# Local attention: the clip of the row sums becomes a maximum over pairs, and the token shift moves from VectorE to ScalarE and GpSimd

## The reference, cut to what matters

```python
def shift_token(t):                       # the upper 64 features come from the token before
    t1, t2 = jnp.split(t, 2, axis=-1)
    t2 = jnp.pad(t2, ((0, 0), (1, 0), (0, 0)))[:, :-1]
    return jnp.concatenate([t1, t2], axis=-1)

def l2norm(t):
    return t / jnp.clip(jnp.linalg.norm(t, axis=-1, keepdims=True), 1e-12)
...
h = shift_token(x)
qkv = h @ wqkv                            # 128 -> 3 x 512, 8 heads of 64
q = l2norm(q) * qs
k = l2norm(k) * ksc
q, k = rotary_xpos(q, k)
o = local_attention(q, k, v)              # windows of 64, each sees itself and the one before
x = x + o @ wo
```

## Time and profile before

| | |
|---|---|
| time of three runs, median (lowest to highest) | 1549.52 us (1544.6 to 1549.98) |
| the profiled execution | 1545.77 us, its span 1544.0 us |
| busy in the span | PE 1237.7 us (80%), DVE 1138.3 us (74%), ACT 865.4 us (56%), POOL 829.3 us (54%) |
| mean granted PE clock | 0.914 |

### The profile page before, as it was taken

How to read it: one execution, slowest core, us unless ns; L and a number is a source line. 1 busy time by engine, 2 the same in 40 slices (tenths; PEclk the granted TensorE clock), 3 DMA queues, 4 the chain that set the end, 5 groups by cost and what they waited for, 6 DMA issues and landing times. The chain is left out here.

```text
span 1544.0 us, 26296 instructions
## 1 busy us (share of the span) xinstructions
PE 1237.7 (80%) x7828; PEld 800.8 (52%) x7828; DVE 1138.3 (74%) x2560; ACT 865.4 (56%) x2259; POOL 829.3 (54%) x760
## 2 busy tenths in 40 slices
PE   6889999854228988479689988885877998898797
PEld 3333333353116877334257666663555766666465
DVE  1299999847118877356589999982658999999464
ACT  5623333243114544237578878783746887888664
POOL 0064344245750555541177767676746776777663
PEclk9999999967559999869889999997998999999999
DMA  3700000031120122130100000000000000000001
GB/s 113 251 1 0 1 0 1 0 104 44 49 90 1 42 63 65 47 120 1 50 1 3 2 1 1 0 1 1 1 22 1 2 2 2 1 1 1 1 1 55
DMA packets 35031, 44.06 MB, mean 29 GB/s; under 512 B 5621, under 2 KB 24978, under 8 KB 34913
## 3 DMA queue, kind: packets, MB, share of 16 engines
q1 hardware_dynamic: 30304, 34.27, 7.0%
q0 software_dynamic: 4608, 8.47, 1.7%
HBM read 22.65 MB, written 21.12 MB: 28 GB/s over the span
## 5 line engine op out<-in xcount | busy, mean ns | idle before, releaser
L1865 ACT ACTIVATE W<-W,nm 128x128 f32<-128x128 f32 x512 | 197.9, 393 | 0.0
L1648 POOL TENSOR_TENSOR W<-W,rden 128x512 f32<-128x512 f32 x128 | 133.0, 1040 | 117.7 <-DVE rden L1966 111.5
L1633 POOL TENSOR_TENSOR R<-R 128x512 f32<-128x512 f32 x128 | 162.6, 1292 | 34.8 <-DVE R L1936 34.8
L1936 DVE TENSOR_TENSOR R<-bank,tab 128x1024 f32<-128x1024 f32 x128 | 151.0, 1214 | 17.0 <-ACT sq L1831 13.1
L1959 DVE CUSTOM_DVE_ANT_0 W<-bank,mask_q,rn 128x128 f32<-128x128 f32 x512 | 146.3, 338 | 7.7 <-issue 4.2
L1194 POOL DMA_INDIRECT expert_rows<-Yt,xin x80 | 83.2, 1040 | 115.4 <-DVE Yt L1167 89.1
L1849 ACT ACTIVATE QK<-bank 128x512 f32<-128x512 f32 x128 | 75.5, 590 | 68.0 <-PE bank L1720 61.1
L616 DVE TENSOR_TENSOR_SCAN S<-beta,U 128x512 f32<-128x512 f32 x64 | 100.0, 1583 | 0.0
L1865 ACT ACTIVATION_READ_ACCUMULATOR W<-W,nm 128x1 f32 x512 | 98.5, 192 | 0.0
L1770 PE MATMUL bank<-PT,VA 128*64 128x128 f32 (+1 forms) x1024 | 86.3, 262 | 13.9 <-issue 10.9
L1745 PE MATMUL bank<-QK 64*64 64x128 f32 x2048 | 85.8, 282 | 11.6 <-DVE nm L1959 11.3
(11 more groups left out here) (310 smaller groups left out, 3583.3 us busy)
## 6 DMA issues: line engine op xcount, KB each, us to landing
expert_slots<-empty SPq DMA_DIRECT2D x8, 650.0 KB, 6.4
xin<-expert_slots SPq DMA_DIRECT2D x8, 650.0 KB
expert_rows<-empty SPq DMA_DIRECT2D x8, 512.0 KB, 6.7
pair_rows<-expert_rows SPq DMA_DIRECT2D x16, 256.0 KB, 4.2
expert_raw<-w1e_dram SPq DMA_DIRECT2D x9, 256.0 KB, 2.8
expert_raw<-w2e_dram SPq DMA_DIRECT2D x9, 256.0 KB, 3.0
tok<-x_dram SPq DMA_DIRECT2D x8, 256.0 KB, 4.5
out_dram<-tok_out SPq DMA_DIRECT2D x8, 256.0 KB, 2.7
```

The source lines that it names most:

```text
L1633: nc.gpsimd.tensor_tensor(halves[:, :, 0, :, z, :], halves[:, :, 0, :, z, :], halves[:, :, 1, :, 1 - z, :], ALU.add).then_inc(summed, 1)
L1648: nc.gpsimd.tensor_tensor(x, x, scale.to_broadcast([P, 4, P]), ALU.mult).then_inc(scaled, 1)
L1865: m = nc.scalar.activation(x, x, ACT.Exp, scale=-1.0, bias=nm[:, p % RING, j:j + 1], accum_out=den[:, p % RING, j:j + 1])
L1936: nc.vector.tensor_tensor(R[:, i, qk, :, :].rearrange("p c (h d) -> p c h d", d=DH), x, y.to_broadcast([P, 2, HEADS, DH]), ALU.mult).then_ ...
```

## The change: what it does

The row sums of the squares go to a buffer of pairs, `sums`, whose second column is filled once with the constant 1e-24, and the clip becomes a `tensor_reduce` with a maximum over each pair. DVE no longer takes part in the token shift: ACT writes `hs_hi` with two copies, at the end of its tiles t = 0 and t = 1, and POOL writes `hs_lo` with two subtractions, at t = 1 and t = 3, between `mix_values` and `scale_keys`. `shifted` now counts two for each chunk, and PE waits for both. Before the first chunk of a layer ACT and POOL make the shift too.

```diff
+            sums = k.sb(f"sums{l}", [P, 2, 2 * HEADS, 2], ctx=ctx)
...
+                def shift_low(g, par, part):                       # in the stream of GpSimd
+                    hi, lo = hs[0][par], hs[1][par]
+                    early_rows, late_rows = shifted_views(k, here(g))
+                    wait_alone(k, pool, hs_hi, 2 * (g + l) + part + 1)
+                    if part == 0:
+                        nc.gpsimd.tensor_tensor(lo[0:DH, :], early_rows, hi[0:DH, :].bitcast(F32), ALU.subtract).then_inc(shifted, 1)
+                        wait_alone(k, pool, shifted, 2 * (g + l) + 1)
+                    else:
+                        nc.gpsimd.tensor_tensor(later(lo[DH:P, :]), late_rows, later(hi[DH:P, :]).bitcast(F32),
+                                                ALU.subtract).then_inc(shifted, 1)
+                        wait_alone(k, pool, shifted, 2 * (g + l + 1))
+                shift_low(G0, 0, 0)
+                shift_low(G0, 0, 1)
...
                             add_halves(g, t)
                             if t % 2:
                                 mix_values(g, par, t // 2)
+                                shift_low(g + 1, 1 - par, t // 2)
                             scale_keys(g, par, t)
...
-                            pe.wait_ge(shifted, g + 1 + l)
+                            pe.wait_ge(shifted, 2 * (g + 1 + l))
...
+                def shift_high(g, par, part):                      # in the stream of ScalarE
+                    hi = hs[0][par]
+                    early_rows, late_rows = shifted_views(k, here(g))
+                    if part == 0:
+                        need(act, v_mm, NTILE * (g - 1))
+                        nc.scalar.activation(hi[0:DH, :], early_rows, ACT.Copy).then_inc(hs_hi, 1)
+                    else:
+                        nc.scalar.activation(later(hi[DH:P, :]), late_rows, ACT.Copy).then_inc(hs_hi, 1)
+                shift_high(G0, 0, 0)
+                shift_high(G0, 0, 1)
...
                         if rows:
                             keep_rows(*rows, 0)
+                        if project and t < 2:
+                            shift_high(g + 1, 1 - par, t)
...
+                nc.vector.memset(sums[:, :, :, 1:2], CLIP2)        # in the stream of VectorE
-                for part in range(4):
-                    shift_part(G0, 0, part)
...
-                    nc.vector.tensor_reduce(ss[:, i, :], sq[:].rearrange("p q (h d) -> p (q h) d", d=DH), AX.X,
-                                            ALU.add).then_inc(sums_r, 1)
+                    nc.vector.tensor_reduce(sums[:, i, :, 0:1].rearrange("p h o -> p (h o)"),
+                                            sq[:].rearrange("p q (h d) -> p (q h) d", d=DH), AX.X, ALU.add).then_inc(sums_r, 1)
                     dve.wait_ge(sums_r, n + 1)
-                    nc.vector.tensor_scalar(ss[:, i, :], ss[:, i, :], CLIP2, None, ALU.max).then_inc(clipped, 1)
+                    nc.vector.tensor_reduce(ss[:, i, :], sums[:, i, :, :], AX.X, ALU.max).then_inc(clipped, 1)
...
                         if project:
-                            shift_part(g + 1, 1 - par, t)
                             rotate(g, t)
```

More of the change, by code:

```diff
@@ L1908, in _ @@
             def _(dve):
+                nc.vector.memset(sums[:, :, :, 1:2], CLIP2)
                 nc.vector.memset(lnb[:], 0.5 * LN_SHIFT * 0.6931471805599453).then_inc(made, 1)
[L1911 to L1925, removed]
-                for part in range(4):
-                    shift_part(G0, 0, part)
                 def rotate(g, t):
```

## The result

| | before | after |
|---|---|---|
| time of the runs, median (lowest to highest) | 1547.06 us (1543.37 to 1549.98) | 1593.64 us (1591.54 to 1594.28) |
| span of the profiled execution | 1544.0 us | 1592.1 us |
| busy DVE, POOL, ACT | 1138.3, 829.3, 865.4 us | 1042.1, 864.3, 891.7 us |
| mean granted PE clock | 0.914 | 0.902 |

The ratio is 1.030, with a 95% interval of 1.0271 to 1.0329. The direction was forecast; the size was 46.6 us where my sum had 18.8, and the time lies above the range. The prediction called its sum +1.0% because it set a sum on the profiled execution against the median of the runs; against the profiled execution, 1545.8 us, 18.8 us is +1.2%.

A forecast was written before the change was run, and what follows sets the result against it. DVE, busy 39.70 of 40 us, was taken as the bound; +7.65 us per layer, +15.3 for two, and +3.5 for PE's clock on the profiled 1545.8 gave 1564.6, say 1565 us; range 1542 to 1583.

The forecast's parts named there:

- the boundary: From the rotation's start in a chunk's tile 3 to that in the next chunk's tile 0: 8.2 us becomes 11.7.
- T0 to T1: From the rotation's start in tile 0 to that in tile 1 of a chunk: falls from 8.2 us to 7.6.
- the price of PE's clock: Clock falls after PE's pauses at chunk boundaries: 0.7 us each at five boundaries, +3.5 us; bounds 0 and 24.
- The rival with the clock at every boundary: PE's clock falls at every chunk boundary, loss not hidden: +10 to +24 us instead of +3.5, 1571 to 1585; chance 0.17.
- the case of more than 1585: Whole kernel slower than 1585 us, from a wait that the prediction doesn't see; chance 0.05.
- the chain of the keys: Tile 1's keys, scaled after POOL's subtraction 11.15 us after that tile's rotation starts, set tile 3's rotation at 15.85 us after it.
- T1 to T3: From the rotation's start in tile 1 to that in tile 3 of a chunk: falls from 17.64 us to 15.85, -1.8.
- Chunks 0 and 1: A layer's first two chunks, where DVE had time to spare: later keys cost +0.9 us together per layer.
- What lies outside the rotations: Start and end of a layer: +2.3 us for the shift before the first chunk, +1.3 for later last keys.
- Even: Pace inside a chunk falls to PE's and ACT's floor, -3.8 us instead of -2.4 in twelve chunks: 1548 us; chance 0.20.
- hidden: At chunk boundaries `shifted` comes before PE asks, so chunks last 29.9 us instead of 34.0: 1497 us; chance 0.12.
- The clip gains nothing: The new clip on DVE waits for POOL as well: +5 us, 1570, inside the forecast's range; no chance of its own.

The follow-up runs named there:

- e3_low_early: Changed kernel with both low-part subtractions earlier on POOL, after scale_keys of tile 1 and before scale_keys of tile 2: 1520.59 us, ratio 0.9822.
- e4_pe_warm: Changed kernel with 13 matmuls on constants on PE before its wait for `shifted` at a chunk's start: 1585.55 us, ratio 1.0266.
- e9_low0_and_pe_warm: Changed kernel with the first low part behind scale_keys and 13 extra matmuls before PE's wait: 1516.46 us beside 1500.48 for the kernel before, ratio 1.0101.
- e6_low0_after_keys: Changed kernel with only the first low part (t = 1) moved behind scale_keys on POOL: 1578.17 us, ratio 1.0226.
- e1_clip_alone: Kernel before with only the new clip and its buffer of pairs, shift left on DVE: 1517.71 us, ratio 0.9801.
- e2_shift_alone: Changed kernel with the old tensor_scalar clip, so only the shift is moved: 1594.89 us, ratio 1.0297.
- e5_low_before_mix: Changed kernel with shift_low ahead of mix_values on POOL at t = 1 and t = 3: 1576.43 us, ratio 1.0206.

## Why the prediction was wrong, step by step

**Right: the mechanism and its sign.** The bound moved from DVE to POOL's second low part, PE's first matmul of a chunk waits 3.3 us for it (3.2 forecast), the boundary is 12.1 (11.7), the first boundary 9.56 and 9.66 (9.5), T0 to T1 at a full clock 7.52 to 7.7 (7.6), the new clip 0.186 us (0.17). e3_low_early, with the same work on the same engines, shows that the place did it.

**The first step that failed: the price of PE's clock.** I wrote "I take 0.7 each at five boundaries, +3.5", on the ground that ACT's 7.6 hides the first microsecond. By the prediction's own numbers it hides less: PE's tile without output was 7.0, so 0.6 is hidden of a fall's 1.7, and 1.1 is left. The count was off too, since every one of the twelve full chunks holds a tile or a boundary with a mean granted clock of 0.81 to 0.89. In the profiled execution eight of the twelve full chunks have T0 to T1 at 8.68 or more, 1.1 to 1.2 above the same tile at a full clock, and others pay at the boundary (12.79) or in tile 2 (9.11, 9.17). A full chunk took 37.4 us, where the chunks of e4_pe_warm with no fall take 36.15: 1.26 x 12 = 15 us where I had 3.5. e9_low0_and_pe_warm against e6_low0_after_keys gives a like size, 14 us in the full chunks and 19 in all. The rival with the clock at every boundary, to which I gave 0.17, was the nearest, but its 1571 to 1585 lies below 1593.6 as well: what came was the case of more than 1585, to which I gave 0.05, and it came from the two mis-sized terms and not from a wait that I hadn't seen. The Trainium skill's page "TensorE: Matmul & The Clock Gate", section "HAM oscillation — how this bites in real kernels", tells of a kernel that pays for such a wait at every turn of its loop. The trace agrees, with a fall in each of the twelve full chunks, though not always at the boundary.

**The second, as large: the chain of the keys.** T1 to T3 at a full clock was 16.5 instead of 15.85. I took the two rotations as one block of 2.35 us, as in the earlier trace rows. With DVE no longer the bound, the second waits 0.2 to 0.4 us for ACT's second square (915.69 and 917.18, 932.22 and 933.63 above), and all of POOL's chain starts later: its additions begin at T1 + 5.03 instead of + 4.67. The wait ahead of a low part is 0.27 to 0.29, not 0.1, and the keys are scaled at 927.41 = T1 + 11.72 instead of + 11.15. On the chunk boundary the same two items, less 0.19 for the shorter subtraction, are most of what makes it 12.03 at a full clock instead of 11.7. Together (0.65 + 0.33) x 12 = 12 us, where I had nothing for them.

**Mis-sized: the rest.** Chunks 0 and 1 cost 4.0 us more instead of 1.8, above all in tile 2 of chunk 1, 9.98 and 10.09 where it was 7.86: there PE waits 2.66 us for late keys, and then its clock is low. What lies outside the rotations (start, end, between the layers) cost 10.5 instead of 7.2; the first rotation alone starts anywhere from 756.6 to 765.5 us in the traces of these kernels, e9_low0_and_pe_warm apart, so this last term is no more than rough. The sum of the four shortfalls is 11.6 + 11.8 + 2.2 + 3.3 = 28.9, and the span grew by 48.1 where I had 18.8: 29.3. The terms account for all but 0.4 us.

**The rivals.** "Even" and "hidden" fell: T1 to T3 never came near 15.0 in the changed kernel. "The clip gains nothing" fell by its own row. Its converse, that the clip matters, holds only where DVE is the bound: 31 us in e1_clip_alone, nothing in the changed kernel beside e2_shift_alone.

**Open.** Where the clock falls in a given chunk differs from chunk to chunk and from kernel to kernel, and I can't say from these traces which pause of 1.8 or 3.3 us trips it. T1 to T2 costs 0.8 to 0.9 more with ACT's copies (8.79 against 7.92, 8.80 against 7.96). In the changed kernel ACT goes without a gap through the second copy, 923.10 to 923.73, to the square at 923.75 for which DVE's rotation at 924.47 waits, so the copy's 0.63 lies in the way of that rotation; the other 0.2 was not taken apart.

## What to carry to other kernels

When work moves to a less busy engine, look at what stands before it in that engine's order and at who waits for it, not at the busy shares: the same two subtractions were worth 73 us by their places. A value that another engine needs at the head of a chunk belongs where its engine is idle well before, not behind the longest chain of the last tile. When an engine stops being the bound, time its former blocks anew (two instructions that ran as one may come apart), and price a new pause of TensorE with the clock that it costs afterwards. And test halves apart: the half that helped, the clip, was worth 2.0% alone and was buried by the other.

## What the runs showed of the hardware

- A `tensor_scalar` of 16 elements on VectorE took 0.17 us beside an idle GpSimd and up to 1.27 beside its instructions (0.90 in the mean of 64); a `tensor_reduce` of 32 elements took 185 to 189 ns in all 64 cases of the changed kernel.
- GpSimd's subtraction with fp32r output takes 1.27 us for 64 x 512 and 1.09 for 64 x 510 in rows of 255: 64 partitions were no faster than the 1.28 of 128 x 512.
- Work that does nothing, 13 matmuls in a pause of TensorE, made the kernel faster by 1.25% where the other pause was out of the way (1.0101 against 1.0226); where it wasn't, the gain of 0.3% was within the noise.
- Pauses that got 1.4 us shorter (e5_low_before_mix) did not raise the mean granted clock: 0.890 to 0.901 in its four executions, 0.897 to 0.902 in those of the changed kernel.
